# Attention with relative positions on one core: row sums from columns of ones, division after a turn, the token update moved to GpSimd, VectorE's small work spread

## The chip, the cores and the metric

The kernel runs on 1 core of one Trainium2 chip. The metric is the device time of one execution in microseconds (us), less is better. Of the kernel before there are three runs and one profiled execution.

## What is computed

A stack of six stages on x (16 batches of 256 tokens, 128 channels): routed feed-forward, retention, routed feed-forward, then a "positions" layer, plain attention, and the positions layer again. The change touches the positions layer, which is run twice. Its reference, cut to what matters (H = 16 heads of HD = 8 channels, E = 32 experts, K = 4):

```python
x = layernorm(src) * g1 + b1
q, k, v = heads(x @ wq), heads(x @ wk), heads(x @ wv)
ac = einsum('bihd,bjhd->bhij', q, k)
bd = (q . p)[i, i - j + S - 1]            # p: sines and cosines of the distance times wp
att = softmax((ac + bd) * scale, axis=-1)
src = src + einsum('bhij,bjhd->bihd', att, v).reshape(B, S, D) @ wo
x2 = layernorm(src) * g2 + b2
sel = sigmoid(x2 @ sel_w);  scores, idx = top_k(sel, 4)
out = src + sum over the 4 chosen experts of score * relu(x2 @ keys[e]) @ values[e]
# around it: x = x + 0.5 * out(layernorm(x))
```

## The kernel before, in words

`relative_attention` (L2635) is the attention half of the positions layer; `mixture` (L3248) does the experts. The attention half is a pipeline over the 16 batches, written out by hand for each engine. A step `s` of the pipeline has 16 places `n` = 0 to 15, and every engine walks the same places in its own fixed order. In one step four batches are in flight: `start` (layernorm and q, k), `prepare` (v), `attend` (scores and softmax) and `finish` (output of the batch that attended the step before). Steps 2 to 17 attend, so 16 steps of each of the two layers are full; step 18 only finishes the last batch.

What each engine does at place `n`, in this order:

- **TensorE** (`step`, L2922): `related` makes the position terms of head `n + 7` into one of two buffers `ur`, or for every fourth head a band (`reach`, L2819); `scores` (L2828) makes two heads' scores of one half of the rows, 256 + 256 columns, into one of two buffers `sr`, after the softmax of place `n - 2` has freed it (L2830); `small` (L2872) does one piece of the small products; `turn_round` (L2847) transposes the exponentials of place `n - 2`; every fourth place `values` (L2858) makes 16 products of 32 output rows into `y_ps`. A buffer `ur` is refilled only when VectorE (L3075, L3084) has read it, and for bands ScalarE too.
- **VectorE** (`step`, L3187): `rotate` (L3069) or `move_band` (L3078) reads `ur`; `maxima` (L3055) reads the scores; at places 0, 8 and 12 it also copies a turned block (L2952); then `small` (L3092) with the layernorms, the top-4 selection (`GATES`), the places in the experts' lists (`PLACES`) and the ends of the attention.
- **ScalarE** (`step`, L3038): `small` (L2982), the copy of turned exponentials (L2962), the rounding of position terms (L3020), and `exponentials` (L2968): two per place, each with `accum_out`, which leaves the row's sum in `zs` and appears in the trace as a second instruction, ACTIVATION_READ_ACCUMULATOR.
- **GpSimd** (`step`, L3237): `add_forms` (L3202) adds the two rotated parts (VectorE may be two ahead of it, L3074), `rest_of_terms` (L3210) the rounding rest; `small` (L3217) has two roots for layernorms (`lead.root` L2286, `opening.root` L2432) and the indirect DMAs `send` (L2580), eight per batch, that write 12 of the 16 batches' tokens to the experts' lists.
- **SyncE** issues the loads and the round trip through HBM that slides the bands.

The small products of TensorE all go through one PSUM bank, the `desk` (L2664): each fill waits until the one before it is emptied. `AT` and the literal `n ==` give the places. For the finishing batch it is now: place 1 VectorE `reciprocal` of `zs` and its widening to `rz8` (L3140, L3142); place 3 TensorE turns `rz8` (L2878) and ScalarE copies it to `rzb`; place 4 VectorE multiplies `y_ps` by it into `yn` (L3147); place 6 TensorE multiplies by `wo` (L2887) and VectorE adds the tokens to get `s1` (L3152); place 7 statistics of `s1`; place 9 VectorE adds half of `s1` to the tokens `x_b` (L3166). `vm` holds the values of a head in 8 of 32 columns, the other columns are zero.

`plain_attention` (L1675), between the two positions layers, already takes its row sums and its division in the way that the change brings here (L1878, L2082, L2086).

Of the kernel before, what the change touches and what calls it, by code (L numbers as in the profile page):

```python
# [28 lines left out]
P = 128  # L29
# [2182 lines left out]
class Lead:  # L2212
# [133 lines left out]
    def take_values(self, act, i, bank):  # L2346
        if i == 0:
            act.wait_ge(self.vm_zero, 1)
# [286 lines left out]
def relative_attention(nc, tag, x_sb, k, io, w, opening, lead=None):  # L2635
# [7 lines left out]
    with ExitStack() as ctx:  # L2643
        a = Pool_(nc, ctx, tag)
        if lead is None:
# [5 lines left out]
        nm = a.sb("nm", [P, SB, 2])  # L2651
        zs = a.sb("zs", [P, 2, TT, H])
        pr = a.sb("pr", [P, 4, 2, T])
        pts = a.sb("pts", [P, 2, TT, QUAD, T])
        rz, rz8, rzb = a.sb("rz", [P, TT, H]), a.sb("rz8", [P, TT, H, HD]), a.sb("rzb", [P, T])
# [14 lines left out]
        nm_ready, av_done, rz_ready, rz8_ready, yn_ready, rr_ready, rr_hi_ready, rr_lo_ready = [a.sem(n) for n in (  # L2670
            "nm_ready av_done rz_ready rz8_ready yn_ready rr_ready rr_hi_ready rr_lo_ready").split()]
# [128 lines left out]
        def _(pe):  # L2800
# [57 lines left out]
            def values(b, r):  # L2858
# [3 lines left out]
                if r == 0 and later_than(b, 1):  # L2862
                    pe.wait_ge(yn_ready, b[0])
# [8 lines left out]
            def small(it, n):  # L2872
                b, e = new(it), finish(it)
                if n == 3 and e:
                    pe.wait_ge(rz8_ready, e[0] + 1)
                    out = fill(it, "rz")
                    for t in range(TT):
                        mm = nc.tensor.transpose(out[:, t * P:(t + 1) * P],  # L2878
                                                 rz8[:, t, :, :].rearrange("p h d -> p (h d)"), k.ident)
                    mm.then_inc(desk.filled, 1)  # L2880
                if n == VALUES - 3 and prep(it):
                    lead.project_values(pe, prep(it)[0], fill(it, "v")).then_inc(desk.filled, 1)
                if n == VALUES - 1 and e:
                    out = fill(it, "o")
                    pe.wait_ge(yn_ready, e[0] + 1)
# [4 lines left out]
                if n == AT["xt"] and b:  # L2890
                    pe.wait_ge(lead.xn_ready, b[0] * TT + TT)
                    lead.turn_tokens(pe, b[0], fill(it, "xt")).then_inc(desk.filled, 1)
# [29 lines left out]
            def step(it):  # L2922
                if attend(it) and is_first(attend(it)[0]):
                    pe.wait_ge(vm_zero, 1)
# [31 lines left out]
        def _(act):  # L2956
# [11 lines left out]
            def exponentials(b, n):  # L2968
# [4 lines left out]
                if n == 0 and later_than(b, 2):  # L2973
                    act.wait_ge(rz_ready, b[0] - 1)
                for x in range(2):
                    h = head_at(hs + x)
                    from_, sign = (minus[:, n % SB, :], -1.0) if slides(hs + x) else (sr.bank(b, n)[:, x * T:(x + 1) * T], 1.0)
                    last = nc.scalar.activation(pr[:, n % 4, x, :], from_, ACT.Exp, bias=nm[:, n % SB, x:x + 1], scale=sign,  # L2978
                                                accum_out=zs[:, b[1], t, h:h + 1])
                last.then_inc(sr.emptied, 1)  # L2980

            def small(it, n):  # L2982
                b, p, e = new(it), prep(it), finish(it)
                if n == 3 and e:
                    bank = taken(it, "rz")
                    copy(rzb[:, :], bank[:, 0:T]).then_inc(desk.emptied, 1)
# [15 lines left out]
                if n == 9 and e and kept(e):  # L3002
                    opening.normal(act, e[0])
# [48 lines left out]
        def _(dve):  # L3052
# [25 lines left out]
            def move_band(b, hs):  # L3078
# [3 lines left out]
                if e >= 2:  # L3082
# [3 lines left out]
            GATES = {5: opening.gate_inverse, 6: opening.gate_best, 9: opening.gate_index, 10: opening.gate_number, 12: opening.gate_one,  # L3086
                     14: opening.gate_mask}
            KEPT = {5: opening.gate_inverse, 6: opening.gate_best, 9: opening.gate_left, 10: opening.gate_kept}
            PLACES = {6: opening.place_chosen, 9: opening.sum_masks, 10: opening.place_sum,
                      11: opening.place_row}  # L3090

            def small(it, n):  # L3092
# [10 lines left out]
                if n == 12 and it[0] == 0 and not led:  # L3103
                    far.cut(dve, ur_ps[:, 0, :])
                i = placed(it)
                if i is not None:
                    if n == 6:
# [28 lines left out]
                if e:  # L3136
                    i, par = e
                    if n == 1:
                        dve.wait_ge(sr.emptied, sr.done(e, NR - 1))
                        nc.vector.reciprocal(rz[:, :, :], zs[:, par, :, :]).then_inc(rz_ready, 1)  # L3140
                        dve.wait_ge(rz_ready, i + 1)
                        nc.vector.tensor_copy(rz8[:, :, :, :], rz[:, :, :].unsqueeze(3).to_broadcast([P, TT, H, HD]))\  # L3142
                            .then_inc(rz8_ready, 1)
                    if n == VALUES - 3:
                        dve.wait_ge(av_done, (i + 1) * QUAD)
                        dve.wait_ge(desk.emptied, desk.done(it, "rz"))
                        nc.vector.tensor_tensor(yn[:, :], y_ps[:, 0:T], rzb[:, :], ALU.mult).then_inc(yn_ready, 1)  # L3147
                    if n == 6:
# [671 lines left out]
```

## Time and profile before

| | |
|---|---|
| three runs | 2728.84, 2732.15, 2733.09 us; median 2732.15 |
| profiled execution | 2728.11 us, of which the span of the core is 2726.4 us |
| PE (TensorE) | 2436.3 us busy, 89% |
| DVE (VectorE) | 1929.8 us, 71% |
| ACT (ScalarE) | 1581.3 us, 58% |
| POOL (GpSimd) | 1557.1 us, 57% |
| attention half of the positions layer | about 840 to 1391 us and 1930 to 2483 us of the span (names f4a and f6a) |

Busy shares are of the whole span. A duration is that of one instruction with its latency; since the next one starts before it ends, what an engine is occupied by is read from start to start. "Idle before" is put down to what released the engine last.

### The profile page before, as it was taken

The page shows a single profiled execution, that of the slowest core. Times are in us where ns is not written, and L with a number is a line of the kernel's source. Part 1 is how long each engine was busy: PE and PEld are TensorE (multiplying, and loading weights), DVE is VectorE, ACT ScalarE, POOL GpSimd, SP SyncE. Part 2 cuts the span into 40 slices and gives each one's busy share as a digit, 9 for nine tenths or more (in the row PEclk, how much of TensorE's full clock was granted, in tenths as well). Part 3 has the DMA queues.
Part 4 walks back from the last instruction along what each step waited for, and adds up shares of the span by engine and source line. Part 5 has one row for each costly group of instructions (what it writes and reads, how often), then busy time and mean ns, then how long its engine had stood idle before and what let it go on. Part 6 is the DMA issues. An engine that isn't in the chain of part 4 may idle for free. (4 is left out here: it accounts for less than half of the span.)

```text
span 2726.4 us, 59982 instructions
## 1 busy us (share of the span) xinstructions
PE 2436.3 (89%) x19038; PEld 1835.0 (67%) x19038; DVE 1929.8 (71%) x5169; ACT 1581.3 (58%) x4641; POOL 1557.1 (57%) x2343
## 2 busy tenths in 40 slices
PE   7999799799977999999988988999799999998898
PEld 5788677578865777777777335665577777777733
DVE  4554388455546899999876456776589999987645
ACT  2332244333326999999930226777699999993022
POOL 4322666332324678888743655554567888874365
PEclk9999899899998999999999997999899999999999
DMA  3720366370005455555455126553445545445512
GB/s 121 311 82 1 74 141 141 120 301 1 1 22 137 124 137 140 137 136 137 130 186 151 46 62 143 114 111 82 105 130 136 137 135 142 137 127 178 158 53 64
DMA packets 302396, 326.64 MB, mean 120 GB/s; under 512 B 31718, under 2 KB 274150, under 8 KB 294902
## 3 DMA queue, kind: packets, MB, share of 16 engines
q1 hardware_dynamic: 252934, 280.83, 37.9%
q0 software_dynamic: 12288, 25.19, 3.3%
q10 hardware_dynamic: 36864, 16.79, 2.1%
q8 instruction: 157, 2.57, 0.4%
q14 instruction: 153, 1.25, 0.2%
HBM read 133.36 MB, written 185.01 MB: 117 GB/s over the span
## 5 line engine op out<-in xcount | busy, mean ns | idle before, releaser
L2073 DVE TENSOR_REDUCE a_nm<-a_sr 128x2 f32<-128x512 f32 x256 | 166.9, 685 | 69.2 <-PE a_sr L1805 68.2
L3207 POOL TENSOR_TENSOR f4o_kv<-a5b_room 128x256 f32<-128x256 f32 x192 | 140.2, 731 | 107.7 <-DVE a5b_room L3075 102.6
L3207 POOL TENSOR_TENSOR f6o_kv<-a5b_room 128x256 f32<-128x256 f32 x192 | 140.3, 731 | 97.6 <-DVE a5b_room L3075 91.8
L2978 ACT ACTIVATE f6a_pr<-f6a_sr,f6a_nm 128x256 f32<-128x256 f32 x384 | 181.4, 486 | 12.0 <-DVE f6a_nm L3063 10.9
L2978 ACT ACTIVATE f4a_pr<-f4a_sr,f4a_nm 128x256 f32<-128x256 f32 x384 | 181.4, 486 | 9.5 <-DVE f4a_nm L3063 7.8
L3075 DVE TENSOR_TENSOR a5b_room<-f4a_ur,f4a_turn 128x512 f32<-128x512 f32 x192 | 131.2, 684 | 44.1 <-PE f4a_ur L2815 43.7
L2837 PE MATMUL f6a_sr<-all_ks,all_qs 96*128 96x256 bf16 x512 | 144.0, 281 | 13.6 <-ACT f6a_pr L2978 10.1
L2837 PE MATMUL f4a_sr<-all_ks,all_qs 96*128 96x256 bf16 x512 | 143.7, 281 | 13.8 <-ACT f4a_pr L2978 10.4
L3075 DVE TENSOR_TENSOR a5b_room<-f6a_ur,f6l_turn 128x512 f32<-128x512 f32 x192 | 131.5, 685 | 34.4 <-PE f6a_ur L2815 33.9
L2854 PE MATMUL f6a_tr<-all_table,f6a_pr 128*128 128x128 f32 x1024 | 154.8, 274 | 0.0
L2854 PE MATMUL f4a_tr<-all_table,f4a_pr 128*128 128x128 f32 x1024 | 154.7, 273 | 0.0
L3214 POOL TENSOR_TENSOR f6a_rr_lo<-f6o_kv,f6a_rr_hi 128x256 fp32r<-128x256 f32 x192 | 139.9, 738 | 5.3 <-ACT f6a_rr_hi L3020 4.9
L3214 POOL TENSOR_TENSOR f4a_rr_lo<-f4o_kv,f4a_rr_hi 128x256 fp32r<-128x256 f32 x192 | 139.6, 737 | 5.8 <-ACT f4a_rr_hi L3020 5.4
L2842 PE MATMUL f6a_sr<-f6l_pe_hi,f6a_rr_hi 128*128 128x256 f32 x384 | 141.3, 368 | 0.0
L2842 PE MATMUL f4a_sr<-f4a_pe_hi,f4a_rr_hi 128*128 128x256 f32 x384 | 140.8, 367 | 0.0
L2962 ACT ACTIVATE f6a_pts<-f6a_tr 128x512 f32<-128x512 f32 x208 | 124.9, 600 | 6.9 <-PE f6a_tr L2854 4.0
L2962 ACT ACTIVATE f4a_pts<-f4a_tr 128x512 f32<-128x512 f32 x208 | 124.9, 601 | 6.6 <-PE f4a_tr L2854 4.1
L3577 POOL DMA_INDIRECT f4m_back<-slots,a5b_row x96 | 92.5, 963 | 61.5 <-issue 24.0
L3577 POOL DMA_INDIRECT f6m_back<-slots,a5b_row x96 | 92.1, 959 | 60.9 <-issue 26.3
L835 POOL TENSOR_TENSOR f_h_lo<-f_h,f_h_hi 128x512 fp32r<-128x512 f32 x64 | 80.1, 1282 | 74.4 <-ACT f_h L468 74.2
L2854 PEld LDWEIGHTS f6a_tr<-all_table,f6a_pr 128*128 128x128 f32 x1024 | 120.2, 142 | 1.7 <-issue 0.2
L2854 PEld LDWEIGHTS f4a_tr<-all_table,f4a_pr 128*128 128x128 f32 x1024 | 120.0, 142 | 1.6 <-issue 0.2
(672 smaller groups left out, 8481.8 us busy)
## 6 DMA issues: line engine op xcount, KB each, us to landing
slots<-f_zero SPq DMA_DIRECT2D x100, 512.0 KB, 6.1
f4a_slide<-f4o_kv SPq DMA_DIRECT2D x64, 383.0 KB
f6a_slide<-f6o_kv SPq DMA_DIRECT2D x64, 383.0 KB
f4o_kv<-f4a_slide SPq DMA_DIRECT2D x64, 256.0 KB
f6o_kv<-f6a_slide SPq DMA_DIRECT2D x64, 256.0 KB
f4o_src<-slots SPq DMA_DIRECT2D x128, 64.0 KB, 2.2
slots<-f4m_y ACTq DMA_DIRECT2D x128, 64.0 KB, 2.3
f6o_src<-slots SPq DMA_DIRECT2D x128, 64.0 KB, 2.2
```

The source lines that it names most:

```text
L835: nc.gpsimd.tensor_tensor(h1_lo[:, m, :], h1[:, m, :], h1_hi[:, m, :], ALU.subtract).then_inc(h1_ready, 1)
L2073: nc.vector.tensor_reduce(nm[:, r // 2, t, at_:at_ + 2], sr[:, g % SB, :].rearrange("p (x s) -> p x s", x=2), AX.X, ALU.max, negate=True). ...
L2837: mm = nc.tensor.matmul(out, qs[0:ROWS, lead.buffer(b[0]), h, t * P:(t + 1) * P], ks[0:ROWS, lead.buffer(b[0]), h, :], start=True, stop=alone)
L2842: nc.tensor.matmul(out, rr_hi[at], pe_hi[:, :], start=False, stop=False)
L2854: mm = nc.tensor.transpose(ring.bank(b, n // 2)[:, o:o + P], pr[:, n % 4, x, st * P:(st + 1) * P], k.ident)
L2962: return nc.scalar.activation(dst, src_, ACT.Copy)
L2978: last = nc.scalar.activation(pr[:, n % 4, x, :], from_, ACT.Exp, bias=nm[:, n % SB, x:x + 1], scale=sign, accum_out=zs[:, b[1], t, h:h + 1])
L3075: nc.vector.tensor_tensor(tmp[:, o % 2, :, :], ur_ps[:, n % 2, :].rearrange("p (u t) -> p u t", u=2), turn[:, :, :], ALU.mult).then_inc(ur ...
L3207: nc.gpsimd.tensor_tensor(rr[:, o % RAW, :], tmp[:, o % 2, 0, :], tmp[:, o % 2, 1, :], ALU.add)\
L3214: nc.gpsimd.tensor_tensor(rr_lo[:, o % RRS, :], rr[:, o % RAW, :], rr_hi[:, o % RRS, :], ALU.subtract)\
L3577: nc.gpsimd.indirect_dma_start(back[:, n % GB, c, :], None, w.slots, bass.IndirectOffsetOnAxis(ap=opening.row[:, n, c:c + 1], axis=0)).the ...
```

## The change

The softmax's exponentials lose `accum_out`. Instead `vm` gets a column of ones for each head in columns that were zero, so that the 32 rows which `values` makes hold two heads' weighted sums (16 rows) and their two row sums; heads r = 0, 1 go to the first 256 columns of `y_ps`, r = 2, 3 to the second. ScalarE copies `y_ps` to SBUF, TensorE turns it (four transposes), VectorE takes the reciprocals and divides on the turned result, TensorE turns it back (two), ScalarE copies. The update of the tokens goes from one VectorE instruction to two on GpSimd. `wo`, `s1`, its statistics, root, normalization, `x2t`, `sel` and the steps of `GATES` and `PLACES` get other places.

```diff
@@ Lead.clear
-        nc.vector.memset(self.vm[:, :, :, :, :].rearrange("p a b c d -> p (a b c d)"), 0.0).then_inc(self.vm_zero, 1)
+        whole = self.vm[:, :, :, :, :]
+        nc.vector.memset(whole.rearrange("p a b c d -> p (a b c d)"), 0.0).then_inc(self.vm_zero, 1)
+        dve.wait_ge(self.vm_zero, 1)
+        for first in (16, 2 * C):
+            nc.vector.memset(bass.AP(whole.tensor, whole.offset + first, [list(whole.ap[0]), [QUAD * C, 2 * TT], [C + 1, 2],
+                                                                         [QUAD * HD, QUAD]]), 1.0).then_inc(self.vm_zero, 1)
@@ relative_attention: the desk's order and the places
-                    [("count", 5, SENT), ("counts", B + 1, 1), ("table", B + 2, 1), ("rz", 3, B), ("v", 1, B), ("o", 3, B),
-                     ("ends", B + 1, 1), ("xt", 0, B), ("qk", 0, B), ("x2t", 3, B),
+                    [("count", 5, SENT), ("counts", B + 1, 1), ("table", B + 2, 1), ("v", 1, B), ("yt", 3, B), ("yb", 3, B),
+                     ("ends", B + 1, 1), ("xt", 0, B), ("o", 3, B), ("qk", 0, B), ("x2t", 3, B),
                      ("sel", 3, B)], 1)
-        AT = {"xt": 8, "qk": 10, "x2t": 12, "sel": 14, "src": 11, "ln": 3}
+        AT = {"y": 4, "yt": 5, "yb": 7, "xt": 8, "o": 9, "qk": 10, "x2t": 14, "sel": 15, "src": 11, "ln": 3}
@@ TensorE
-                        mm = nc.tensor.matmul(y_ps[q, 0:T], vm[:, b[0] % 2, st, r, q], pts[:, r % 2, st, j, :],
+                        mm = nc.tensor.matmul(y_ps[q, r // 2 * T:(r // 2 + 1) * T], vm[:, b[0] % 2, st, r, q], pts[:, r % 2, st, j, :],
-                if n == 3 and e:
-                    pe.wait_ge(rz8_ready, e[0] + 1)
...
-                if n == VALUES - 1 and e:
...
+                if n == AT["yt"] and e:
+                    pe.wait_ge(y_copied, e[0] + 1)
+                    out = fill(it, "yt")
+                    for hf in range(2):
+                        for t in range(TT):
+                            o = (hf * TT + t) * P
+                            mm = nc.tensor.transpose(out[:, o:o + P], y_sb[:, hf, t * P:(t + 1) * P], k.ident)
+                    mm.then_inc(desk.filled, 1)
+                if n == AT["yb"] and e:
+                    pe.wait_ge(yq_ready, e[0] + 1)
+                    out = fill(it, "yb")
+                    for t in range(TT):
+                        mm = nc.tensor.transpose(out[:, t * P:(t + 1) * P], yq[:, t, :], k.ident)
+                    mm.then_inc(desk.filled, 1)
+                if n == AT["o"] and e:
+                    pe.wait_ge(desk.emptied, desk.done(it, "yb"))
...
@@ ScalarE
-                if n == 0 and later_than(b, 2):
-                    act.wait_ge(rz_ready, b[0] - 1)
-                    last = nc.scalar.activation(pr[:, n % 4, x, :], from_, ACT.Exp, bias=nm[:, n % SB, x:x + 1], scale=sign,
-                                                accum_out=zs[:, b[1], t, h:h + 1])
+                    last = nc.scalar.activation(pr[:, n % 4, x, :], from_, ACT.Exp, bias=nm[:, n % SB, x:x + 1], scale=sign)
-                if n == 3 and e:
-                    bank = taken(it, "rz")
-                    copy(rzb[:, :], bank[:, 0:T]).then_inc(desk.emptied, 1)
+                if n == AT["y"] and e:
+                    act.wait_ge(av_done, (e[0] + 1) * QUAD)
+                    if e[0]:
+                        act.wait_ge(yq_ready, e[0])
+                    copy(y_sb[:, :, :].rearrange("p h t -> p (h t)"), y_ps[:, :]).then_inc(y_copied, 1)
+                if n == AT["yb"] and e:
+                    copy(yn[:, :], taken(it, "yb")[:, 0:T]).then_inc(desk.emptied, 1)
-                if n == 9 and e and kept(e):
+                if n == 12 and e and kept(e):
                     opening.normal(act, e[0])
@@ VectorE
-            GATES = {5: opening.gate_inverse, 6: opening.gate_best, 9: opening.gate_index, 10: opening.gate_number, 12: opening.gate_one,
-                     14: opening.gate_mask}
+            GATES = {5: opening.gate_inverse, 6: opening.gate_best, 9: opening.gate_index, 10: opening.gate_number, 13: opening.gate_one,
+                     15: opening.gate_mask}
-            PLACES = {6: opening.place_chosen, 9: opening.sum_masks, 10: opening.place_sum,
-                      11: opening.place_row}
+            PLACES = {2: opening.place_chosen, 4: opening.place_sum, 6: opening.place_row,
+                      7: opening.sum_masks}
+                if n == 0 and 0 <= i < B - 1:
+                    dve.wait_ge(desk.emptied, desk.done((it[0] - 1, (it[1] + 1) % 2), "sel"))
+                    opening.gate_sum(dve, i)
-                    if n == 1:
...
-                    if n == VALUES - 3:
...
+                    if n == AT["yt"]:
+                        dve.wait_ge(desk.filled, desk.nth(it, "yt"))
+                        bank = desk.bank(it, "yt").rearrange("p (h g c) -> p h g c", h=2, c=QUAD * HD)
+                        for hf in range(2):
+                            last = nc.vector.reciprocal(rz[:, hf, :, :], bank[:, hf, :, 16 * (1 - hf):16 * (1 - hf) + 2])
+                        last.then_inc(rz_ready, 1)
+                        dve.wait_ge(rz_ready, i + 1)
...
+                        for hf in range(2):
+                            last = nc.vector.tensor_tensor(
+                                yq[:, :, :].rearrange("p t (j c) -> p (t j) c", c=QUAD * HD)[:, :, 16 * hf:16 * hf + 16]
+                                .rearrange("p g (r d) -> p g r d", d=HD),
+                                bank[:, hf, :, 16 * hf:16 * hf + 16].rearrange("p g (r d) -> p g r d", d=HD),
+                                rz[:, hf, :, :].unsqueeze(3).to_broadcast([P, 2 * QUAD, 2, HD]), ALU.mult)
+                        last.then_inc(yq_ready, 1)
...
-                    if n == 6:
+                    if n == AT["o"]:
...
+                            dve.wait_ge(halved, i)
-                    if n == 7:
+                    if n == AT["o"] + 1:
-                    if n == 9:
-                        nc.vector.scalar_tensor_tensor(x_b[:, i, :, :], s1[:, :, :], 0.5, x_b[:, i, :, :],
-                                                       ALU.mult, ALU.add)
-                    if n == 15 and kept(e):
-                        dve.wait_ge(desk.emptied, desk.done(it, "sel"))
-                        opening.gate_sum(dve, i)
@@ GpSimd
-                if e and n == 7 and kept(e):
+                if e and n == 10 and kept(e):
                     opening.root(pool, e[0])
+                if e and n == 15:
+                    pool.wait_ge(opening.s1_aggr, e[0] + 1)
+                    if e[0]:
+                        pool.wait_ge(x_moved, e[0])
+                    nc.gpsimd.tensor_scalar(half[:, :, :], s1[:, :, :], 0.5, None, ALU.mult).then_inc(halved, 1)
+                    pool.wait_ge(halved, e[0] + 1)
+                    nc.gpsimd.tensor_tensor(x_b[:, e[0], :, :], x_b[:, e[0], :, :], half[:, :, :], ALU.add).then_inc(x_moved, 1)
```

## Rows read from the trace of the kernel before

**Rows 1.** The page's part 1: busy us, share of the span, instructions.

```profile
PE 2436.3 (89%) x19038; PEld 1835.0 (67%) x19038; DVE 1929.8 (71%) x5169; ACT 1581.3 (58%) x4641; POOL 1557.1 (57%) x2343
```

**Rows 2.** Stretches: us, then busy of PE, PEld, DVE, ACT, POOL, PEclk, DMA share, GB/s.

```profile
1087.00:1288.00 201.00, 185.04 (x1689) 147.87 (x1688) 187.46 (x523) 188.65 (x624) 164.22 (x237) 1.00 0.50 136
...
920.00:954.50 34.50, 32.55 (x294) 25.50 (x292) 30.20 (x88) 32.79 (x110) 20.53 (x34) 1.00 0.47 123
```

**Rows 3.** Timeline of VectorE, two steps' addition of the tokens: start us, us, engine line.

```profile
1161.61 0.40 DVE L3152 TENSOR_TENSOR f4o_s<-f4a_desk,f4o_src 128x256 f32<-128x256 f32 x1
...
1196.08 0.40 DVE L3152 TENSOR_TENSOR f4o_s<-f4a_desk,f4o_src 128x256 f32<-128x256 f32 x1
```

**Rows 4.** Waits in the stretch 1087:1288: us in total, times, longest us.

```profile
POOL f4o_kv L3207 <- DVE a5b_room L3075: 23.2, 33, 1.4
PEld f4a_ur L2815 <- DVE f4o_kv L3084: 12.5, 11, 1.7
PE f4a_ur L2815 <- DVE f4o_kv L3084: 9.9, 11, 1.5
...
PEld f4a_ur L2825 <- DVE a5b_room L3075: 5.2, 13, 0.7
...
PEld f4a_sr L2837 <- ACT f4a_pr L2978: 4.1, 7, 0.7
```

**Rows 5.** Timeline of VectorE in one step, around places 1 and 2, 4, 9 and 10.

```profile
1185.01 0.34 DVE L3140 RECIPROCAL f4a_rz<-f4a_zs 128x32 f32<-128x32 f32 x1
...
1185.97 0.54 DVE L3084 COPY f4o_kv<-f4a_ur 128x383 f32<-128x383 f32 x1
...
1191.21 0.42 DVE L3147 TENSOR_TENSOR f4a_yn<-f4a_y,f4a_rzb 128x256 f32<-128x256 f32 x1
...
1203.16 1.30 DVE L3166 SCALAR_TENSOR_TENSOR all_x<-f4o_s,all_x 128x256 f32<-128x256 f32 x1
1204.39 0.54 DVE L3084 COPY f4o_kv<-f4a_ur 128x383 f32<-128x383 f32 x1
```

**Rows 6.** Timeline of ScalarE: one exponential, its accumulator read, the next exponential.

```profile
1183.12 0.48 ACT L2978 ACTIVATE f4a_pr<-f4a_sr,f4a_nm 128x256 f32<-128x256 f32 x1 [0.44 <-DVE f4a_nm L3063]
1183.49 0.19 ACT L2978 ACTIVATION_READ_ACCUMULATOR f4a_pr<-f4a_sr,f4a_nm 128x1 f32 x1
1183.58 0.50 ACT L2978 ACTIVATE f4a_pr<-f4o_kv,f4a_nm 128x256 f32<-128x256 f32 x1
```

**Rows 7.** Timeline of TensorE: two transposes of `rz8` and what starts after them.

```profile
1187.75 0.38 PE L2878 MATMUL f4a_desk<-all_table,f4a_rz 128*128 128x128 f32 x2
1187.97 0.60 PE L2854 MATMUL f4a_tr<-all_table,f4a_pr 128*128 128x128 f32 x4
```

**Rows 8.** Plain attention: timeline of VectorE's division; ScalarE's copy (min/median/max ns).

```profile
1774.76 0.36 DVE L2082 RECIPROCAL a_rz<-a_desk 128x16 f32<-128x16 f32 x2
...
1775.56 0.68 DVE L2073 TENSOR_REDUCE a_nm<-a_sr 128x2 f32<-128x512 f32 x1
...
L1940 ACT ACTIVATE a_y_sb<-a_y x16: 597/597/597, 1676.4 to 1913.7; 128x512 f32<-128x512 f32 x16
```

**Rows 9.** One line's instructions each: ns min/median/max, first and last start, form.

```profile
L3207 POOL TENSOR_TENSOR f4o_kv<-a5b_room x192: 714/730/754, 832.6 to 1369.8; 128x256 f32<-128x256 f32 x192
...
L3589 POOL COPY f4m_staged<-f4o_kv x128: 288/293/348, 1394.3 to 1469.2; 128x128 f32 x128
...
L2138 POOL TENSOR_SCALAR a_xn<-all_x,a5b_mv,a5b_rstd x28: 782/794/798, 1636.9 to 1846.3; 128x128 f32<-128x128 f32 x28
...
L3166 DVE SCALAR_TENSOR_TENSOR all_x<-f4o_s,all_x x16: 417/1301/1320, 892.8 to 1390.3; 128x256 f32<-128x256 f32 x16
```

**Rows 10.** Timeline at the end of the first positions layer's attention.

```profile
1387.41 0.42 DVE L3147 TENSOR_TENSOR f4a_yn<-f4a_y,f4a_rzb 128x256 f32<-128x256 f32 x1 [1.56 <-PE f4a_y L2867]
...
1390.33 0.42 DVE L3166 SCALAR_TENSOR_TENSOR all_x<-f4o_s,all_x 128x256 f32<-128x256 f32 x1
...
1392.86 1.09 PE L3331 MATMUL f4m_x_ps<-all_table,f4o_src 128*128 128x128 f32 x4 [4.20 <-PEq L83]
```

More of the change, by code:

```diff
@@ L2650, in relative_attention @@
         qs, ks = k.qs, k.ks
-        nm = a.sb("nm", [P, SB, 2])
-        zs = a.sb("zs", [P, 2, TT, H])
+        nm, half = a.sb("nm", [P, SB, 2]), a.sb("half", [P, TT, C])
         pr = a.sb("pr", [P, 4, 2, T])
         pts = a.sb("pts", [P, 2, TT, QUAD, T])
-        rz, rz8, rzb = a.sb("rz", [P, TT, H]), a.sb("rz8", [P, TT, H, HD]), a.sb("rzb", [P, T])
+        y_sb, rz, yq = a.sb("y_sb", [P, 2, T]), a.sb("rz", [P, 2, 2 * QUAD, 2]), a.sb("yq", [P, TT, C])
         tmp = w.room[:, 0:2 * 2 * TT, :].rearrange("p (n u t) c -> p n u (t c)", n=2, u=2)
@@ L2664, in relative_attention @@
         desk = Desk(a.ps("desk", [P, 1, 512]), a.sem("desk_filled"), a.sem("desk_emptied"),
[L2665 to L2666 removed]
+                    [("count", 5, SENT), ("counts", B + 1, 1), ("table", B + 2, 1), ("v", 1, B), ("yt", 3, B), ("yb", 3, B),
+                     ("ends", B + 1, 1), ("xt", 0, B), ("o", 3, B), ("qk", 0, B), ("x2t", 3, B),
                      ("sel", 3, B)], 1)
[L2668 removed]
+        AT = {"y": 4, "yt": 5, "yb": 7, "xt": 8, "o": 9, "qk": 10, "x2t": 14, "sel": 15, "src": 11, "ln": 3}
         ur_ps, ur_filled, ur_turned, ur_moved = a.ps("ur", [P, 2, 512]), a.sem("ur_filled"), a.sem("ur_turned"), a.sem("ur_moved")
[L2670 to L2671 removed]
+        nm_ready, av_done, rz_ready, y_copied, yq_ready, rr_ready, rr_hi_ready, rr_lo_ready, x_moved, halved = [a.sem(n) for n in (
+            "nm_ready av_done rz_ready y_copied yq_ready rr_ready rr_hi_ready rr_lo_ready x_moved halved").split()]
         free = opening.kv[:, 1, :, :].rearrange("p e c -> p (e c)")
@@ L2873, in small @@
                 b, e = new(it), finish(it)
-                if n == 3 and e:
-                    pe.wait_ge(rz8_ready, e[0] + 1)
[L2876 to L2880, printed above, removed]
                 if n == VALUES - 3 and prep(it):
                     lead.project_values(pe, prep(it)[0], fill(it, "v")).then_inc(desk.filled, 1)
-                if n == VALUES - 1 and e:
+                if n == AT["yt"] and e:
[12 more added lines that the diff above has]
+                    mm.then_inc(desk.filled, 1)
+                if n == AT["xt"] and b:
+                    pe.wait_ge(lead.xn_ready, b[0] * TT + TT)
+                    lead.turn_tokens(pe, b[0], fill(it, "xt")).then_inc(desk.filled, 1)
+                if n == AT["o"] and e:
+                    pe.wait_ge(desk.emptied, desk.done(it, "yb"))
                     out = fill(it, "o")
-                    pe.wait_ge(yn_ready, e[0] + 1)
                     for t in range(TT):
@@ L2889, in small @@
                     mm.then_inc(desk.filled, 1)
-                if n == AT["xt"] and b:
-                    pe.wait_ge(lead.xn_ready, b[0] * TT + TT)
-                    lead.turn_tokens(pe, b[0], fill(it, "xt")).then_inc(desk.filled, 1)
                 if n == AT["qk"] and b:
@@ L3137, in small @@
                     i, par = e
-                    if n == 1:
-                        dve.wait_ge(sr.emptied, sr.done(e, NR - 1))
-                        nc.vector.reciprocal(rz[:, :, :], zs[:, par, :, :]).then_inc(rz_ready, 1)
-                        dve.wait_ge(rz_ready, i + 1)
-                        nc.vector.tensor_copy(rz8[:, :, :, :], rz[:, :, :].unsqueeze(3).to_broadcast([P, TT, H, HD]))\
-                            .then_inc(rz8_ready, 1)
-                    if n == VALUES - 3:
[L3145 to L3148, printed above, removed]
+                    if n == AT["yt"]:
[4 more added lines that the diff above has]
+                        last.then_inc(rz_ready, 1)
+                        dve.wait_ge(rz_ready, i + 1)
+                        if i:
+                            dve.wait_ge(desk.filled, desk.nth((it[0] - 1, (it[1] + 1) % 2), "yb"))
+                        for hf in range(2):
[5 more added lines that the diff above has]
+                        last.then_inc(yq_ready, 1)
+                        dve.wait_ge(yq_ready, i + 1)
+                        dve.sem_inc(desk.emptied, 1)
+                    if n == AT["o"]:
                         dve.wait_ge(desk.filled, desk.nth(it, "o"))
```

9 lines of the change are left out of this document (5 added, 4 removed).

## The prediction, made before the changed kernel ran

> **What bounds the kernel now.** The page's busy shares [rows 1] say little: TensorE has 89% of the whole span, but the change lies in two stages of some 550 us each. I therefore read the steady stretch of the first of them, 201 us long [rows 2]. The batches follow each other there by 1196.08 - 1161.61 = 34.47 us [rows 3]; the steady steps around it give 34.45, which I use. So the stretch holds 201/34.45 = 5.83 steps, and the busy time of a step is TensorE 31.7 us, ScalarE 32.3, VectorE 32.1, GpSimd 28.2, with TensorE's granted clock at 1.00 (2.4 GHz) throughout. Three engines are at 92 to 94% at once: none alone is the bound, each waits for the others in turn. The earlier stretch of one step, before the lists of tokens begin [rows 2], has the same 34.5 us although VectorE has 30.2 us and GpSimd only 20.5 of it; ScalarE has 32.8, TensorE 32.6. There these two set the pace.
>
> The waits tell where TensorE, which the change loads least, loses time [rows 4]. Before its weight loads it waits, per step, 12.5/5.83 = 2.1 us for VectorE's band copy, 5.2/5.83 = 0.9 for its rotation, and 4.1/5.83 = 0.7 for ScalarE's exponentials: 3.7 us together. By its own work it would need 34.45 - 3.7 = 30.7 us. (From its matmuls' busy time it is 31.7; that counts the latency of the last matmul before each wait, so I take the lower.) The band waits have a visible cause: at place 9 VectorE is held by the update of the tokens from 1203.16 to 1204.39, and only then does the band copy start [rows 5]; at place 1 it is held from 1185.01 to 1185.97 by the reciprocal and its widening, again just ahead of a band copy.
>
> **The change, part by part**, per step.
>
> *ScalarE.* The accumulator read starts at 1183.49 and the next exponential at 1183.58 [rows 6]: 32 x 0.09 = 2.9 us go. That is the least; if the exponential itself gets shorter without the sum, it could be 32 x 0.15, for it starts 0.37 us before its read. I take 2.9, which the rows show. Added: the copy of `y_ps`, 0.60 us, as plain attention's [rows 8]; the copy of the turned-back result has the shape of the `rzb` copy that goes. Net -2.3: 32.3 becomes 30.0 us. The new copy at place 4 waits for the last `values` (place 3) and has `take_values` and the exponentials of place 4 behind it.
>
> *VectorE.* Removed: 1185.97 - 1185.01 = 0.96, the product 0.42, the update 1204.39 - 1203.16 = 1.23 [rows 5], 2.6 us in all. Added: the division, 1775.56 - 1774.76 = 0.8 us with its inner wait, as plain attention does it [rows 8]. Net -1.8: 30.3 us. The other moves cost nothing by themselves. They take 1 us and more each from the places ahead of the band copies at 2 and 10; the division's 0.8 us goes to place 5, ahead of the band copy at 6, and I count that in what is kept of the band waits below. The two extra memsets run once per layer.
>
> *TensorE.* Two transposes go, six come; two take 1187.97 - 1187.75 = 0.22 us [rows 7], so +0.44. `values` keeps its 16 products per group. Own work: 30.7 + 0.44 = 31.2 us (rounded up).
>
> *GpSimd.* The sum, 0.73 us [rows 9], and the halving. No row has a one-input product of this shape: the 128-column copy took 0.29, the least it can be; the 128-column product and sum with two scalars took 0.79, so twice that, 1.59, is the most. I take 0.75, near the sum of equal width. With 0.1 between the two that is 1.6 us. GpSimd waits 23.2/5.83 = 4.0 us for rotations now [rows 4], so it is occupied 30.5 us and would be 32.1. Its root moves to place 10 and waits there for VectorE's statistics of that place, with a `send` and the next `add_forms` behind it; VectorE may be two rotations ahead, so 3 us of it are covered. If that cover is gone it shows as VectorE waiting at L3075.
>
> The Trainium skill speaks against this part: GPSIMD Engine Reference, section 4.1, sends elementwise work to VectorE and calls GpSimd about 2 times slower for two inputs, one input near line rate. By it the halving would cost about as much as an equal copy, an estimate near 0.5 us, and the sum above would move by 0.25 us in the change's favour; the 0.73 us row for two inputs against VectorE's shortest 0.42 agrees with the first half.
>
> *The desk.* One bank now serves `yb`, `xt`, `o`, `qk` at places 7, 8, 9, 10 and `x2t`, `sel`, `count` at 14, 15, 0, each waiting for a reader one place back. Readers on ScalarE have gained time. The tightest is `qk`: it waits for VectorE's sum of place 9. I put 0.2 us on these waits, between 0 (a place is 2 us) and 1.2, the length of the longest piece moved; behind each stand the turns and scores of TensorE. SyncE's queue gets nothing; its band transfers are released by copies that come earlier.
>
> *The ends.* The last batch has a longer chain: a copy 0.6, four and two transposes 0.6, the division 0.8 in place of a product 0.42, a copy 0.4, GpSimd's pair 1.6 in place of 0.42: up to 3.5 us. Today the update starts at 1390.33 and the next stage's first matmul at 1392.86 [rows 10]. Part may be hidden by the experts' weights; 0 to 3.5, I take 2.5, twice.
>
> **The sum.** Of today's 3.7 us of waits I let ScalarE's 0.7 go, keep the 0.9 for rotations, keep a quarter (0.5) of the band's, since both pieces that held it are gone or halved, and add 0.2 for the desk: 1.6 us. The step is 31.2 + 1.6 = 32.8 us, 1.65 less. Sixteen steps attend in each layer: 32 x 1.65 = 52.8, less 5 at the ends, is 47.8 us. From the profiled execution's 2728.1 this gives 2680.3; the runs' median is 4.0 above it, so 2684. Measurement tells about 0.2% (5.5 us) from no change.
>
> **The cases.**
>
> 1. *Forecast* (0.53): TensorE sets the pace at 32.2 to 33.4 us a step, 2665 to 2704.
>
> 2. *The waits nearly vanish* (0.15): 0.6 left, a step of 31.8: 32 x 2.65 - 5 = 80, 2652 us. For it: four engines then have slack of their own. Against: all four are still above 90%.
>
> 3. *GpSimd becomes the bound* (0.15): the halving costs 1.59, GpSimd is occupied 30.5 + 2.4 = 32.9 us, with 0.8 of waits 33.7. That holds for the 12 of 16 steps of a layer that send (96 sends of 8 a step); the others gain as forecast. 24 x 0.75 + 8 x 1.65 - 5 = 26, 2706 us.
>
> 4. *It does not do what it says* (0.07): the accumulator read was hidden work, the exponentials keep their pace, and ScalarE goes to 32.9 us. Since the early stretch moved at 34.5 us with ScalarE at 32.8 [rows 2], the step stays at 34.3, the ends eat the rest: 2732 us. Against it: the start-to-start times of rows 6.
>
> 5. *Slower: the two engines collide* (0.10). VectorE's update took 0.417 us where GpSimd was still and 1.301 in the median [rows 9], so reading the same memory beside GpSimd costs 3.1 times. If the same stretch hits GpSimd's sum and the halving is 1.59, the pair costs 1.59 + 3.1 x 0.73 = 3.9 us at place 15, GpSimd is occupied 34.4 us, with 0.8 of waits 35.2, and the rotations wait for it. 24 x 0.75 = 18 slower, 13 faster in the other steps, 5 at the ends: 2742 us. It decides from a pair of about 3.2 us upward. Against: no GpSimd sum of that width ran over 0.754 in the 192 of rows 9.
>
> The Trainium skill has the rule for this case: SBUF — State Buffer, section "Who interferes with whom", says that a VectorE instruction with two SBUF inputs and a GpSimd one that reads SBUF take a shared port pair in turn, the second blocked until the first ends. By that rule the update on VectorE paid for GpSimd's reads, in agreement with 1.301 against 0.417, and taking it away returns the stretch too, which the 1.23 us above already has.
>
> The likeliest case gives 2684. The range of 8 in 10 reaches from 2652 (half of case 2) to 2712 (all of case 3). Faster by over 0.2%: cases 1 to 3, 0.83. Within: case 4, 0.07. Slower: 0.10.
>
> **What would show it.** Right: steps of about 32.8 us between additions of the tokens; no accumulator reads for the exponentials; ScalarE near 30 us a step; band waits of TensorE under 1 us a step; GpSimd's halving under 1 us. Wrong: VectorE waiting for GpSimd before L3075's successor, or TensorE before `qk` or `count` for the desk by more than 0.5 us a step; a busy time of TensorE a step that grew by more than 0.5 us; exponentials that start 0.46 us apart as now.

## The result: 0.8% slower, and the profile after

| | before | after |
|---|---|---|
| median of four runs each | 2732.62 us | 2755.64 us |
| span of the profiled execution | 2726.4 us | 2755.1 us |

The ratio is 1.0083, with a 95% interval of 1.0066 to 1.0101. The forecast was 2684 us, the range 2652 to 2712: the sign was wrong. The profile page's part 1 of the kernel after:

```profile
PE 2446.3 (89%) x19166; PEld 1850.5 (67%) x19166; DVE 1923.1 (70%) x5173; ACT 1513.9 (55%) x3649; POOL 1597.6 (58%) x2407
```

Its stretches, with the columns of [rows 2]:

```profile
1087.00:1288.00 201.00, 186.84 (x1724) 150.90 (x1717) 187.84 (x522) 175.04 (x440) 172.05 (x251) 1.00 0.51 138
920.00:953.00 33.00, 32.34 (x296) 25.92 (x295) 29.25 (x90) 29.87 (x77) 21.76 (x35) 1.00 0.46 125
```

Its waits in the stretch 1087:1288:

```profile
PEld f4a_ur L2819 <- DVE f4o_kv L3095: 12.2, 11, 1.6
POOL f4o_kv L3225 <- DVE a5b_room L3086: 10.4, 12, 1.6
...
PEld f4a_ur L2829 <- DVE a5b_room L3086: 7.4, 10, 0.9
...
POOL f4o_veps L2442 <- DVE f4o_mv L3187: 6.2, 6, 1.0
```

Against [rows 1, 2], ScalarE and GpSimd moved as forecast: ScalarE's busy time fell by 67 us, GpSimd's rose by 41. But a steady step takes as long as before, 34.55 us against 34.45 (here 1195.42 - 1160.87):

```profile
1160.87 0.40 DVE L3176 TENSOR_TENSOR f4o_s<-f4a_desk,f4o_src 128x256 f32<-128x256 f32 x1
...
1195.42 0.41 DVE L3176 TENSOR_TENSOR f4o_s<-f4a_desk,f4o_src 128x256 f32<-128x256 f32 x1
```

The stretch holds 201/34.55 = 5.82 steps, and TensorE's wait for the band copy, which was to fall from 2.1 us a step to 0.5, is still 12.2/5.82 = 2.1. Only the first steps, before the lists of tokens begin, got shorter: 33.26, 32.94 and 33.47 us where they were 33.98, 34.55 and 33.79.

Landmarks of TensorE divide the whole difference (starts in the two traces, us; "the last `values`" is the start of the last group of 16 products):

| stretch | before | after | difference |
|---|---|---|---|
| start to the first scores of layer 1 | 839.6 | 836.6 | -3.0 |
| first scores to the last `values` of layer 1 | 546.8 | 545.4 | -1.4 |
| last `values` to the experts' first matmul | 6.6 | 18.4 | +11.8 |
| from there to the first scores of layer 2 | 534.8 | 542.1 | +7.3 |
| first scores to the last `values` of layer 2 | 549.9 | 548.9 | -1.1 |
| last `values` to the experts' first matmul | 6.8 | 18.6 | +11.8 |
| from there to the end | 241.9 | 245.1 | +3.2 |

The sum is +28.6 us; the spans differ by 28.7. So there are two questions: where the steps' gain went, and what takes 11.8 us at each end.

**The steps.** The timeline of the kernel after at places 13 and 14, VectorE and GpSimd:

```profile
1169.30 0.74 POOL L3225 TENSOR_TENSOR f4o_kv<-a5b_room 128x256 f32<-128x256 f32 x1
...
1169.44 2.27 DVE L2531 TENSOR_TENSOR f4o_one<-all_table,f4o_number 128x256 f32<-128x256 f32 x1
...
1170.00 1.41 POOL L3232 TENSOR_TENSOR f4a_rr_lo<-f4o_kv,f4a_rr_hi 128x256 fp32r<-128x256 f32 x2
...
1171.62 0.55 DVE L3095 COPY f4o_kv<-f4a_ur 128x383 f32<-128x383 f32 x1
```

`gate_one`, the comparison that moved from place 12 to 13, takes 2.27 us. One line's instructions, after and before:

```profile
L2531 DVE TENSOR_TENSOR f4o_one<-all_table,f4o_number x12: 570/2273/2305, 929.6 to 1307.6; 128x256 f32<-128x256 f32 x12
```

```profile
L2526 DVE TENSOR_TENSOR f4o_one<-all_table,f4o_number x12: 415/416/418, 933.5 to 1313.3; 128x256 f32<-128x256 f32 x12
```

It ends at 1171.71, 0.30 us after the third of three unbroken GpSimd instructions (1171.41). Behind it stands the band copy, for which TensorE's next weight load waits 1.61 us:

```profile
1172.22 0.11 PEld L2819 LDWEIGHTS f4a_ur<-all_qs,all_ws 96*128 96x128 bf16 x2 [1.61 <-DVE f4o_kv L3095]
```

The comparison runs in 12 of the 16 steps of a layer, and those are the ones that gained nothing.

**The ends.** The timeline of the kernel after at the end of the first attention half:

```profile
1388.99 0.85 POOL L3243 TENSOR_SCALAR f4a_half<-f4o_s 128x256 f32<-128x256 f32 x1 [12.36 <-DVE f4o_mv L3187]
1389.92 0.72 POOL L3245 TENSOR_TENSOR all_x<-all_x,f4a_half 128x256 f32<-128x256 f32 x1
1399.50 0.34 SPq L1567 DMA_DIRECT2D a5b_room<-in_w  x1
1399.60 0.19 POOL L2442 TENSOR_TENSOR f4o_veps<-f4o_mv,all_half 128x2 f32<-128x2 f32 x1 [8.95 <-POOLq L83]
...
1400.42 0.45 PE L3356 MATMUL f4m_x_ps<-all_table,f4o_src 128*128 128x128 f32 x1 [13.10 <-PEq L83]
```

Nothing is computed or issued from 1390.64 to 1399.50. The views leave out instructions that compute nothing; the trace's own records have GpSimd's DRAIN, an instruction of its sequencer, ahead of the barrier that ends a stage. Its record can start before GpSimd's last instruction does (kernel, start us, duration us, end us, GpSimd's last instruction and its end):

```
before  1372.71  10.68  1383.39  send L2585, 1374.61
after   1389.88   8.69  1398.57  token update L3245, 1390.64 (last send 1374.89)
before  2464.01  10.36  2474.37  send L2585, 2465.90
after   2499.20   8.68  2507.88  token update L3245, 2499.96 (last send 2484.05)
```

Before, the drain ran beside the last batch's output and was over 7 us before VectorE's last update ended (1390.75 by [rows 10]), so it cost nothing. Now the token update of the last batch is GpSimd's last work, so the drain starts 17 us later (its 8.7 us contain the last addition), and everything waits for its end at 1398.6, 7.9 us after that addition.

### The profile page after: what moved, and what is told of

Read it like the earlier page. It is cut to its first block and busy times, and to the rows that moved or that the text cites. A ratio compares the mean times of both kernels' runs of the same rounds, so it can differ in the third digit from the quotient of the medians.

```text
span 2755.1 us, 59436 instructions
## 1 busy us (share of the span) xinstructions
PE 2446.3 (89%) x19166; PEld 1850.5 (67%) x19166; DVE 1923.1 (70%) x5173; ACT 1513.9 (55%) x3649; POOL 1597.6 (58%) x2407
## 5 line engine op out<-in xcount | busy, mean ns | idle before, releaser
L2986 ACT ACTIVATE f6a_pr<-f6a_sr,f6a_nm 128x256 f32<-128x256 f32 x384 | 171.3, 491 | 28.0 <-DVE f6a_nm L3074 22.8
L2986 ACT ACTIVATE f4a_pr<-f4a_sr,f4a_nm 128x256 f32<-128x256 f32 x384 | 171.1, 490 | 23.6 <-DVE f4a_nm L3074 18.5
L3602 POOL DMA_INDIRECT f4m_back<-slots,a5b_row x96 | 92.4, 962 | 68.3 <-DVE f4m_kept L3558 26.4
L3602 POOL DMA_INDIRECT f6m_back<-slots,a5b_row x96 | 91.8, 957 | 66.0 <-issue 28.7
```

The source lines that it names most:

```text
L3602: nc.gpsimd.indirect_dma_start(back[:, n % GB, c, :], None, w.slots, bass.IndirectOffsetOnAxis(ap=opening.row[:, n, c:c + 1], axis=0)).the ...
```

## The experiments

Each was timed beside the kernel before on the same chip, e1 to e8 on one and e9 to e11 on another; the kernel before had medians of 2733.4 us (beside e1 to e4), 2733.6 (e5 to e8) and 2731.6 (e9 to e11). A difference in us between runs of different groups can be off by 2 us for that. "Step" is the median distance of two token sums in the steps with lists, where 34.45 is before and 34.55 after.

### 1 and 2. Each suspect taken away alone, and both

```diff
@@ e1: gate_one back at place 12
-GATES = {5: opening.gate_inverse, 6: opening.gate_best, 9: opening.gate_index, 10: opening.gate_number, 13: opening.gate_one,
+GATES = {5: opening.gate_inverse, 6: opening.gate_best, 9: opening.gate_index, 10: opening.gate_number, 12: opening.gate_one,
@@ e2: the last batch's update on VectorE; e3: both edits
-                if e and n == 15:
+                if e and n == 15 and e[0] < B - 1:
...
+                    if n == AT["o"] + 1 and i == B - 1:
+                        nc.vector.scalar_tensor_tensor(x_b[:, i, :, :], s1[:, :, :], 0.5, x_b[:, i, :, :],
+                                                       ALU.mult, ALU.add)
```

> The changed kernel with one edit: gate_one, VectorE's comparison of 128x256 with two SBUF inputs, goes back from place 13 to place 12. Theory A (collision): in the changed kernel it takes 2.27 us in the median where it took 0.42 before, since GpSimd runs three 0.73 us additions in a row beside it, and the band copy of place 14 behind it holds TensorE for 1.6 us. At place 12 it meets an indirect DMA of GpSimd instead and takes 0.4 to 0.6 us; the 24 steps that have it lose 1.0 to 1.6 us each, 24 to 38 us: 2718 to 2732 us, and steps of 33.0 to 33.6 us. Theory B (GpSimd or the sum of the engines sets the step, GpSimd being occupied 31.9 of 34.55 us): the comparison gets short but the wait moves elsewhere, steps stay above 34.2 us, 2748 to 2756 us.

Measured: 2731.55 us, ratio to before 1.0000 (0.9987 to 1.0014), 24 us less than the kernel after; step 33.48. The comparison has a median of 415 ns. At the edge of A's range, and B is refuted. The wait for the band copy, 12.2 us in the stretch 1087:1288 of the kernel after, is here:

```profile
PEld f4a_ur L2819 <- DVE f4o_kv L3095: 3.9, 6, 1.2
```

> The changed kernel with one edit: only the last batch of each layer has its token update on VectorE (one instruction after the statistics), the other 15 stay on GpSimd. Theory A (GpSimd's drain): at the end of the layer GpSimd's DRAIN takes 8.7 us and cannot start before its last instruction; before the change it started at 1372.9 and ran beside the last batch's output, in the changed kernel it starts at 1389.9 and everything waits for it. Without the last update it starts some 14 us earlier and is hidden again: 8 to 9 us less at each end, 2736 to 2741 us. Theory B (the longer chain of the last batch is what costs): it goes by the 1.6 us of the pair less the 0.4 of the one instruction, 1 us at each end, 2752 to 2756 us.

Measured: 2739.14 us, ratio 1.0017 (1.0003 to 1.0031), 16.5 us less than after; step 34.57. As A.

> Both edits of the two runs before this one in the changed kernel. If collision and drain are independent, their savings add: 24 to 38 and 15 to 19 us, 2699 to 2717 us, and the kernel is faster than before the change by 0.5 to 1.2 per cent. If what they free is taken by GpSimd as the bound, it stays above 2730 us.

Measured: 2714.08 us, ratio 0.9925 (0.9897 to 0.9953), step 33.49. The savings add (24.1 + 16.5 = 40.6; measured 41.6). TensorE's timeline at the end of the layer in this kernel:

```profile
1374.23 1.07 PE L2871 MATMUL f4a_y<-f4a_pts,f4a_vm 128*32 128x256 f32 x16 [0.78 <-ACT f4a_pts L2973]
...
1378.78 0.68 PE L2901 MATMUL f4a_desk<-f4a_wo,f4a_yn 128*128 128x128 f32 x4 [0.56 <-ACT f4a_yn L2973]
1383.22 1.09 PE L3359 MATMUL f4m_x_ps<-all_table,f4o_src 128*128 128x128 f32 x4 [3.76 <-PEq L83]
```

From the last `values` to the experts 9.0 us, against 6.6 before: the longer division chain costs 2.4 us, and the drain was the other 9.4 of the 11.8.

### 3. The drain by itself, in the kernel before

```diff
@@ e5, the kernel before
-                    if n == 9:
+                    if n == 9 and i < B - 1:
...
+                if e and n == 9 and e[0] == B - 1:
+                    pool.wait_ge(opening.s1_aggr, B)
+                    nc.gpsimd.tensor_scalar(half[:, :, :], s1[:, :, :], 0.5, None, ALU.mult).then_inc(halved, 1)
+                    pool.wait_ge(halved, 1)
+                    nc.gpsimd.tensor_tensor(x_b[:, e[0], :, :], x_b[:, e[0], :, :], half[:, :, :], ALU.add)
```

> The kernel before with one edit: the token update of the last batch of each layer (one of 16) goes to GpSimd as two instructions, the other 15 stay on VectorE. Theory A (GpSimd's drain): its last instruction ends at about 1391.5 in place of 1372.7, the drain of 8.7 us then begins there, and the next stage starts 8 to 9 us later: 2748 to 2751 us. Theory B (the ends cost only the pair's own 1.6 us): 2734 to 2737 us.

Measured: 2751.36 us, ratio 1.0072 (1.0055 to 1.0090): 17.8 us for four instructions of GpSimd in the whole program, 0.4 us above A's range; B is refuted. Its drains start at 1389.67 and 2494.95 and take 8.67 each. The timeline:

```profile
1389.71 0.72 POOL L3225 TENSOR_TENSOR all_x<-all_x,f4a_half 128x256 f32<-128x256 f32 x1
1399.27 0.34 SPq L1567 DMA_DIRECT2D a5b_room<-in_w  x1
```

### 4. Whose collision it is: place, root or pair

Four kernels have the comparison at place 13: the kernel before with it there (e4), the kernel after, one with GpSimd's root of the second layernorm at place 11 (e10), and one without any token update on GpSimd (e11).

```diff
@@ e4, the kernel before; e10 = e8 (below), e11 = e7 (below), each with this line
-GATES = {5: opening.gate_inverse, 6: opening.gate_best, 9: opening.gate_index, 10: opening.gate_number, 12: opening.gate_one,
+GATES = {5: opening.gate_inverse, 6: opening.gate_best, 9: opening.gate_index, 10: opening.gate_number, 13: opening.gate_one,
```

> The kernel before with one edit: gate_one from place 12 to place 13, nothing else. Theory A (collision by place): GpSimd runs three additions in a row at that place too (1176.9 to 1178.9 in the trace of before), so the comparison takes 1.5 to 2.3 us in place of 0.42, ahead of the band copy of place 14; 24 steps lose 0.5 to 1.4 us, 2744 to 2766 us. Theory B (the comparison is stretched only because GpSimd got the token update): it stays at 0.42 to 0.7 us and the time within 5 us of 2732.

Measured: 2729.91 us, ratio 0.9994 (0.9983 to 1.0005), the comparison's median 0.62 us. As B.

> The kernel of e7_update_on_vector (no update on GpSimd, its root at place 10) with the comparison back at place 13. Theory A (the pair on GpSimd at place 15 makes the unbroken row of additions): without it the comparison takes 0.4 to 0.9 us, as in the kernel before with it at 13, and the time stays within 8 us of 2715. Theory B (the row comes from the root's wait at place 10): it takes 1.6 to 2.3 us, 2735 to 2755 us.

Measured: 2740.11 us, ratio 1.0034 (1.0018 to 1.0051), 25 us above e7; step 34.62. As B: the row is there without the pair.

> The kernel of e8_root_at_11 with the comparison gate_one back at place 13. Theory A (the collision belongs to the place: whatever runs there meets three additions of GpSimd in a row): it takes 1.6 to 2.3 us again, the 24 steps that have it lose 1.0 to 1.6 us, 2729 to 2743 us. Theory B (it belongs to GpSimd's lateness, which the root's wait at place 10 makes): with the root at 11 GpSimd is elsewhere, the comparison takes 0.4 to 0.9 us and the time stays within 8 us of 2705.

Measured: 2714.66 us, ratio 0.9941 (0.9919 to 0.9962), step 33.44, 10 us above e8. Between the two theories: the root's place changes the price and does not remove it. The comparison's rows in e4, e11 and e10, in this order:

```profile
L2526 DVE TENSOR_TENSOR f4o_one<-all_table,f4o_number x12: 519/622/1507, 934.7 to 1313.3; 128x256 f32<-128x256 f32 x12
```

```profile
L2531 DVE TENSOR_TENSOR f4o_one<-all_table,f4o_number x12: 573/2440/2462, 931.4 to 1314.3; 128x256 f32<-128x256 f32 x12
```

```profile
L2531 DVE TENSOR_TENSOR f4o_one<-all_table,f4o_number x12: 577/1558/2419, 931.7 to 1301.6; 128x256 f32<-128x256 f32 x12
```

So one instruction at one place has four prices, 0.62, 1.56, 2.27 and 2.44 us. It is neither the place alone nor the pair; in every one of these rows it ends 0.3 us after one of GpSimd's instructions, and the price is how many of them pass first. In the kernel after and in e11, VectorE waited for three in a row. In e10 it came in after two, in e4 after one, and then GpSimd paid: there VectorE's comparison ends at 1176.33 and the two subtractions take 1.62 us where two take 1.41 in the kernel after:

```profile
1175.28 0.75 POOL L3207 TENSOR_TENSOR f4o_kv<-a5b_room 128x256 f32<-128x256 f32 x1
...
1175.70 0.63 DVE L2526 TENSOR_TENSOR f4o_one<-all_table,f4o_number 128x256 f32<-128x256 f32 x1
...
1175.98 1.62 POOL L3214 TENSOR_TENSOR f4a_rr_lo<-f4o_kv,f4a_rr_hi 128x256 fp32r<-128x256 f32 x2
```

Why VectorE gets in after the first instruction in e4 and only after the third in the kernel after, though GpSimd's instructions follow each other as closely in both, stays open. The traces show a difference in phase: in the steady steps the comparison starts 0.42 us after the first of the additions in e4, 0.17 in e10, 0.13 in the kernel after and 0.05 before it in e11, in the order of the prices. But in the first steps with lists 0.12 us ended after two instructions and 0.14 after one, so phase alone is not shown to decide it.

### 5. What the rest of the change is worth

All of these start from e3.

```diff
@@ e6: the sums of the exponentials again, into a tile that nobody reads
-bias=nm[:, n % SB, x:x + 1], scale=sign)
+bias=nm[:, n % SB, x:x + 1], scale=sign,
+                                                accum_out=zs[:, b[1], t, h:h + 1])
@@ e7: all token updates on VectorE, at place 11, none on GpSimd
+                    if n == 11:
+                        nc.vector.scalar_tensor_tensor(x_b[:, i, :, :], s1[:, :, :], 0.5, x_b[:, i, :, :],
+                                                       ALU.mult, ALU.add)
@@ e8: GpSimd's root at place 11, ScalarE's normalization at 13; e9: e7 and this
-                if e and n == 10 and kept(e):
+                if e and n == 11 and kept(e):
                     opening.root(pool, e[0])
...
-                if n == 12 and e and kept(e):
+                if n == 13 and e and kept(e):
                     opening.normal(act, e[0])
```

> The kernel of e3_both with one edit: the exponentials get their accum_out back, into a tile that nobody reads. It costs ScalarE 32 accumulator reads a step, 2.9 us of issue. Theory A (in this kernel GpSimd and VectorE hold the step, GpSimd being occupied 32.4 of 33.5 us, ScalarE about 30): the reads cost nothing or up to 0.4 us a step, 2714 to 2727 us. Theory B (the removal of the reads is what brought the steps from 34.5 to 33.5): 0.8 to 1.2 us a step comes back, 2740 to 2752 us.

Measured: 2738.27 us, ratio 1.0018 (1.0007 to 1.0030), 24 us above e3; step 34.06, and in the steps without lists 34.06 in place of 32.95. A is refuted and the time is 2 us under B's range; a step gains back 0.57 us with lists, less than B's 0.8, and 1.1 without. The profiled execution was the fastest of its ten (2727.21); between the two traces the attention stages differ by 17 us. In its stretch 1087:1288 the longest wait of TensorE's weight loads is for ScalarE, where e3 has 2.8 us of it:

```profile
PEld f4a_sr L2841 <- ACT f4a_pr L2987: 12.2, 23, 0.7
```

> The kernel of e3_both with one edit: all token updates on VectorE, one instruction at place 11 (0.42 us alone, up to 1.3 beside GpSimd's additions), none on GpSimd. Theory A (GpSimd holds the step of 33.5 us): it is relieved of 1.6 us, the step goes to 32.6 to 33.0 us, 32 steps save 16 to 29 us: 2685 to 2700 us. Theory B (VectorE holds it): the 0.4 to 1.3 us more on VectorE make the step 33.6 to 34.2 us, 2717 to 2737 us.

Measured: 2715.15 us, ratio 0.9934 (0.9916 to 0.9952), step 33.61. The step is at the lower edge of B's, the time 2 us under B's range: relieving GpSimd of 1.6 us and loading VectorE with one instruction cancel out. That instruction takes 0.99 us here, beside an indirect DMA of GpSimd (it ends at 1061.31, 0.32 us after it):

```profile
1059.96 1.03 POOL L2590 DMA_INDIRECT slots<-f4o_x,a5b_row  x1 [0.16 <-issue]
...
1060.32 0.99 DVE L3189 SCALAR_TENSOR_TENSOR all_x<-f4o_s,all_x 128x256 f32<-128x256 f32 x1
```

> The kernel of e3_both with one edit: GpSimd's root of the second layernorm goes from place 10, where GpSimd waits 1.0 us a step for VectorE's statistics of the same place, to place 11, ScalarE's normalization from 12 to 13. Theory A (GpSimd holds the step): its only wait goes, the step becomes 32.5 to 32.9 us, 2688 to 2704 us. Theory B (TensorE with VectorE hold it): the step stays within 0.2 us of 33.5, 2708 to 2720 us.

Measured: 2704.95 us, ratio 0.9907 (0.9890 to 0.9925), the fastest of all; step 33.05, a little above A's range, the time 1 us above it. GpSimd's 1.0 us a step of waiting for the statistics is gone from the trace, and TensorE's wait for rotations fell from 11.6 us in the stretch (e3) to 6.2, so that wait was on the path. The edit moves ScalarE's normalization too; the two were not tried apart.

> The kernel of e8_root_at_11 with all token updates on VectorE at place 11, as in e7_update_on_vector. There the update took 0.99 us in the steady steps. Theory A (with the root at 11 GpSimd still holds the step of 33.05 us): taking its 1.6 us away gives 32.6 to 32.9 us, 2690 to 2700 us. Theory B (TensorE and VectorE hold it now, GpSimd waits again 1.1 us a step for rotations): VectorE's 1.0 us more makes the step 33.2 to 33.7 us, 2708 to 2722 us, and the update is better placed on GpSimd.

Measured: 2707.02 us, ratio 0.9914 (0.9887 to 0.9941), step 33.06. Neither: GpSimd has 1.6 us less to do and the step is the same, so GpSimd no longer sets it alone. Nor was VectorE tested as B meant: the update took 0.42 us there (median), not the 0.99 of e7. In the stretch 1087:1288 of e8, of 201/33.05 = 6.08 steps, TensorE is nearest to its limit, busy 195.4/6.08 = 32.1 of 33.05 us; that it is the bound was not tried.

```profile
1087.00:1288.00 201.00, 195.40 (x1795) 158.18 (x1793) 186.45 (x553) 181.71 (x463) 181.73 (x262) 1.00 0.54 144
```

## Why the prediction was wrong, by its steps

*What bounds the kernel* held in the main. ScalarE had a part in the early steps: with its reads back they take 34.06 us, without 32.95 (e6 against e3). Of the 2.9 us only 1.1 count there; without the reads TensorE is nearest to the step (busy 32.34 of 33.00 us in the stretch 920:953 of the kernel after). In the later steps e6 gives 0.57 us of the 2.9, as the account of several engines side by side would have it.

*ScalarE* was right: a read costs 0.09 us between exponentials, ScalarE came to 175.04/5.82 = 30.1 us a step, forecast 30.0. Case 4, that the reads are hidden work, is refuted by e6: they are worth 24 us by the medians.

*VectorE* is the step that failed: "The other moves cost nothing by themselves." I costed the moved comparison by its duration at its old place. It has two inputs in SBUF, the same kind as the update, whose stretch from 0.417 to 1.301 us I had in [rows 9] and used for the update only. With it VectorE came to 187.84/5.82 = 32.3 us, forecast 30.3: the comparison took 1.85 us more and the sum of the masks 0.3 (623 ns in place of 327). And it landed right ahead of a band copy: the very wait I let shrink to 0.5 us had its two causes removed and got a third. The forecast gave that wait back by naming what went away from it, without asking what newly stood there. With the comparison out of the way the wait was what I had forecast: 3.3 us in the stretch of e3, 0.55 a step. Cost: 24 us (e1).

*GpSimd*: the sum 0.73 as forecast, the halving 0.86, forecast 0.75 (both at the end of the layer above). The Trainium skill (GPSIMD Engine Reference, section 4.1) calls one input "roughly line-rate", from which the prediction had an estimate of 0.5; the trace does not agree, with more for one input than for the two of the sum. Less its waits it is occupied 33.05 - 6.3/6.08 = 32.0 us in e8, forecast 32.1. Case 3, GpSimd as the bound, asked for 33.7 us a step. e3 ran at 33.49 and gained 0.44 us when GpSimd's wait was taken away (e8), so GpSimd was part of that bound, through the root's wait that I took as covered by VectorE being two rotations ahead. Cost: 9 us (e8 against e3); in e3 TensorE waits 11.6 us in the stretch for rotations, 1.9 a step where I kept 0.9.

*The ends* failed too: 2.5 us each was the chain alone. The chain of the last batch was sized well: 2.5 us taken, 2.4 and 2.4 measured (9.0 and 9.2 in e3 against 6.6 and 6.8). Missing was the drain, 9.4 us twice. [Rows 10] had the sign of it that I did not read: the gap from the update to the next stage was put down to a barrier, and I did not ask which engine arrives there last, and with what. Cost: 16.5 us (e2), 17.8 (e5).

*The desk* (0.2 us): no wait of TensorE for it appears among those of the stretch after. *Case 5*, the collision, had the right resource and the wrong victim: GpSimd's sum stayed at 0.73 us, VectorE's comparison paid. Its 2742 us came nearest, by another sum.

*The sum.* With both hazards out and the root moved, a step is 33.05 us, forecast 32.8; e8's 2705 us would have been in the range. TensorE's weight loads wait there 6.2 us in the stretch for rotations, 4.5 for exponentials and 3.1 for bands, 13.8/6.08 = 2.3 us a step where I kept 1.6: own work is 30.8, forecast 31.2, and ScalarE's 0.7 us, which I let go, is still there. Of the 21 us between e8 and the forecast, 32 x 0.25 = 8 are the step. The rest is mostly that I gave every step the gain of a steady one: in layer 1 of e8 the first three distances of token sums gained 0.7, 1.5 and 0.7 us, and the thirteenth and fourteenth 0.8 and -0.7, not 1.65 each. The two attention stages of the traces became 17.7 and 16.1 us shorter (TensorE's first scores to last `values`), where 16 x 1.65 = 26.4 was forecast for each. Together: the kernel after lies 72 us above the forecast, of which 42 are the two hazards (e3), 9 the root's wait (e8) and 21 this.

*Not settled.* The experts' stage and what follows took 7.3 and 3.2 us more in the kernel after, though its code is the same. From its first matmul to that of plain attention the three kernels with the attention of before have 242.1, 242.7 and 244.9 us, the nine runs of the new one between 242.5 and 247.8, the kernel after 249.6; these are single executions, and no run isolates it.

## What to carry to other kernels

A moved instruction keeps its price only if what runs beside it keeps still: for each VectorE instruction with two inputs in SBUF, look at what GpSimd does at the new place, and what stands behind it. Before giving an engine the last work of a stage, look at how it leaves the stage. One instruction on GpSimd can cost 9 us there, and the same on VectorE nothing. When removing what stands before a wait, list everything that will stand there after.

## What the runs showed of the hardware

- GpSimd's DRAIN took 8.2 to 11.8 us at the end of every stage in which it had issued indirect DMAs (52 drains in the 13 profiles). Its record often starts before GpSimd's last instruction; counted from that instruction's end, 48 of the 52 ended 7.9 us later and four, in the kernel before and e4, 8.3 to 8.8. It was 7.9 whether the last instruction was an indirect DMA or an addition 16 us after the last send (kernel after, 1374.89 to 1390.64). In stages without indirect DMAs it took at most 0.84 us and ended 0.07 us after the last instruction (kernels before and after). That the indirect DMAs are its cause was not tried.
- A VectorE instruction with two SBUF inputs does not only wait for the GpSimd instruction that it meets. It can wait for three unbroken ones: 2.27 and 2.44 us in place of 0.42, its end each time 0.3 us after the last of them. The Trainium skill (SBUF — State Buffer, "Who interferes with whom") calls the port pair that the two engines share "an exclusive lock" and says "Issue order, not op shape, decides who blocks." The trace agrees for one instruction (e4: 0.62 us) and shows more for the row of three.
- An indirect DMA of GpSimd can hold such a VectorE instruction as well: in e7 the updates that started 0.36 us into one took 0.97 to 1.00 us. It does not always: in the kernel before, the comparisons that started 0.14 to 0.17 us into one took 0.42.
